# Rows sent to their experts place by place: POOL's later sends held until PE has turned the rows of an earlier expert

## The reference, cut to what matters

```python
x = x + L0_xattn(layernorm(x), ...)          # int8-like quantised expert linear
x = x + L0_ffn(layernorm(x), ...)            # weights looked up in a table of 16
x = x + L1_xattn(ctx, layernorm(x), ...)     # a state-space scan
x = x + L1_ffn(layernorm(x), ...)            # mixture of experts, below

probs = softmax(x @ gate_w)                  # 32 experts; 2048 rows
w, sel = top_k(probs, 8);  w = w / sum(w)
# every row goes to its 8 experts; an expert takes its rows in order, up to its capacity
y = (silu(xg @ w_gate[e]) * (xg @ w_up[e])) @ w_down[e]
out[row] += w * y
```

## Time and profile before

| | us |
|---|---|
| timed runs, median of 3 | 2109.94 |
| timed runs, lowest and highest | 2106.46, 2112.08 |
| the profiled execution, its own time | 2116.83 |
| the profiled execution, its span | 2115.0 |
| routing, sends and experts (last block) | 1225 to 2115 |
| POOL's 128 sends, first and last start | 1258.5, 1431.6 |
| PE busy, DVE busy, ACT busy, POOL busy | 1535.6, 1441.8, 903.5, 679.5 |

### The profile page before, as it was taken

One profiled execution on the slowest core, in us unless ns is written; L12 is line 12 of the kernel. 1 busy time (PEld: TensorE's weight loads), 2 busy tenths in 40 slices (PEclk: granted clock), 3 DMA queues, 4 the chain that ended last, 5 costly groups with the idle time before them and its releaser, 6 DMA issues. The chain is left out here.

```text
span 2115.0 us, 26326 instructions
## 1 busy us (share of the span) xinstructions
PE 1535.6 (73%) x9312; PEld 1305.2 (62%) x9312; DVE 1441.8 (68%) x2096; ACT 903.5 (43%) x1579; POOL 679.5 (32%) x450
## 2 busy tenths in 40 slices
PE   5767787774599699699689352106999999998930
PEld 3444454443589589589689341105888899997820
DVE  6676786864898998998999362003666655558854
ACT  3535555453444544544544140003655566665510
POOL 1010100101544644654554136770000000008876
PEclk9879788976699799799799775557999999999965
DMA  7888798744637338437435045654668666669877
GB/s 226 290 284 299 243 360 306 270 145 146 249 130 292 150 125 295 162 117 277 167 131 179 20 166 203 248 209 134 199 200 287 209 210 210 210 209 329 271 220 232
DMA packets 167496, 455.04 MB, mean 215 GB/s; under 512 B 17328, under 2 KB 19376, under 8 KB 157632
## 3 DMA queue, kind: packets, MB, share of 16 engines
q1 hardware_dynamic: 90880, 280.11, 39.7%
q10 hardware_dynamic: 56000, 106.06, 13.6%
q0 software_dynamic: 20480, 67.13, 9.3%
HBM read 271.83 MB, written 181.40 MB: 214 GB/s over the span
## 5 line engine op out<-in xcount | busy, mean ns | idle before, releaser
L1116 POOL TENSOR_TENSOR mix_st<-mix_Bb,mix_du 128x2048 f32<-128x2048 f32 x64 | 293.2, 4582 | 272.0 <-DVE mix_st L1399 260.2
L1391 DVE TENSOR_TENSOR_SCAN mix_st<-mix_dA,mix_st 128x512 f32<-128x512 f32 x256 | 311.9, 1218 | 42.8 <-POOL mix_st L1116 22.2
L1800 POOL DMA_INDIRECT moe_gat<-x_by_expert,moe_where x128 | 160.8, 1256 | 509.9 <-DMA x_by_expert<-moe_ys 471.5
L1264 ACT ACTIVATE mix_dA<-mix_dt,mix_A 128x512 f32<-128x512 f32 x256 | 177.0, 692 | 263.6 <-DVE mix_st L1391 259.8
L1187 PE MATMUL mix_G<-mix_xThi,mix_wup 128*128 128x256 f32 x1408 | 266.0, 287 | 15.6 <-issue 14.7
L1924 PE MATMUL moe_G<-moe_xhi,moe_whi 128*128 128x288 f32 x768 | 234.9, 306 | 11.0 <-issue 11.0
L1187 PEld LDWEIGHTS mix_G<-mix_xThi,mix_wup 128*128 128x128 f32 x1408 | 226.6, 196 | 18.5 <-issue 17.1
L1924 PE MATMUL moe_G<-moe_xhi,moe_wlo 128*128 128x288 f32 x768 | 229.1, 298 | 9.6 <-issue 9.6
L1924 PE MATMUL moe_G<-moe_xlo,moe_whi 128*128 128x288 f32 x768 | 229.4, 299 | 9.0 <-issue 8.9
L427 PE MATMUL front_L<-front_oh,front_pick 128*128 128x512 f32 x528 | 176.1, 470 | 45.4 <-ACT front_wst L574 28.9
L1213 PE MATMUL mix_Y<-mix_ident,mix_st 128*128 128x128 f32 x1024 | 145.9, 298 | 86.4 <-DVE mix_st L1399 86.3
(11 more groups left out here) (235 smaller groups left out, 3238.6 us busy)
## 6 DMA issues: line engine op xcount, KB each, us to landing
x_by_expert<-front_zeros ACTq DMA_DIRECT2D x16, 4096.0 KB, 20.4
mix_wup<-w_halves SPq DMA_DIRECT2D x44, 1024.0 KB, 5.6
moe_raw<-in_ew SPq DMA_DIRECT2D x32, 1280.0 KB
moe_xt<-x_by_expert SPq DMA_DIRECT2D x128, 256.0 KB
x_by_expert<-moe_ys ACTq DMA_DIRECT2D x128, 256.0 KB
mix_wdn<-w_halves SPq DMA_DIRECT2D x44, 512.0 KB, 6.5
front_idx<-in_idx SPq DMA_DIRECT2D x44, 384.0 KB, 8.6
w_halves<-front_wst SPq DMA_DIRECT2D x44, 384.0 KB, 7.5
```

Of the source, the lines that this page charges most:

```text
L1116: nc.gpsimd.tensor_tensor(st[:, g % STBUF, :, :], Bb[:, q, :, :], du[:, k % 2, :].unsqueeze(1).to_broadcast([P, NG, S]), ALU.mult).then_in ...
L1264: nc.scalar.activation(dA[:, :], dt[:, k % 2, :], ACT.Exp, scale=A[:, c, m:m + 1]).then_inc(da_ready, 1)
L1391: nc.vector.tensor_tensor_scan(r, dA[:, :], r, 0.0, ALU.mult, ALU.add).then_inc(scanned, 1)
L1800: pool.indirect_dma_start(out=gat[:, q, :], out_offset=None, in_=s["XG"], in_offset=bass.IndirectOffsetOnAxis(ap=where[:, i, k:k + 1], axi ...
```

## The change

Ahead of the 16 sends of each place k from 2 to 7, POOL now waits for `xT_ready` to reach NT * (k - 1), which is when PE has transposed all five tiles of expert k-2: 5 for place 2, 10 for place 3, up to 30 for place 7. Nothing else is changed: the sends, their order, the loads and PE's stream are the same.

```diff
--- before.py
+++ after.py
@@ -1784,6 +1784,7 @@
                     for i in range(b * TT, (b + 1) * TT):
                         send(i, k)
             for k in range(2, TOP):
+                pool.wait_ge(xT_ready, NT * (k - 1))
                 for i in range(TILES):
                     send(i, k)
```

## The result

The changed kernel took 2055.6 us (median of 4, 2052.18 to 2062.63) beside 2111.01 us for the kernel before on the same chip: ratio 0.9734, 95% interval 0.9712 to 0.9755, some 55 us less. Forecast were 2081 us and 29 us less, so the gain is nearly twice the forecast one. Two later batches gave the same: 2061.97 beside 2116.06 (0.9733, 0.9710 to 0.9756) and 2063.12 beside 2114.9 (0.9761, 0.9717 to 0.9805).

What follows compares the result with a forecast made beforehand. PE's results, known only one in 2.8 us while POOL sends without a break, bound the kernel. M5 = 1341 + 35.6 + 4 x 33.6 = 1511, 29 us earlier; 2109.94 - 29 = 2081 us, own range 2050 to 2107, over the cases 2015 to 2116.

Steps and rivals of the forecast that it cites:

- M5: Middle of period 5, PE's 64-row transposes: forecast 1511 against 1539.9 before, 29 us earlier; nothing different after it.
- The first rival: POOL's sends: each has its price wherever it stands; M5 = 1543, +3 us, time 2113; no change had 0.14.
- The tail after every burst: Between a place's last send and PE's release stand 12 us, five times: +21 us, 2131; chance 0.14.
- Hardly touched PE: Short bursts at the gathers' price, 22 us a period: M5 = 1451, 89 us earlier, 2021; chance 0.17.
- M0: Middle of period 0, PE's 64-row transposes after place 2's sends: forecast 1341, 107 us before the old one.
- The five periods: PE's work from M0 to M5, places 3 to 7 sent one each: first 35.6 us, then four of 33.6.
- 6 us of full pace: Grace after each start of a place's sends: PE does 40 instructions before its results come late.
- the long train: POOL's unbroken sends in the kernel before, 147 us: PE's results become known one in 2.8 us.
- catching up, tail and dependency: After a place's burst: 8.6 us for PE's remaining work, 2 us tail, 1 us for a dependency not ready.
- The clock: PE after each stop runs at the low clock: 24 matmuls in 5.00 us at 0.56.
- The Trainium skill's rule: DMAs from all engines share 16 DMA engines; held sends cost the same at another time, nothing won.
- a cost of recording the execution: If the hold were only this, the timed kernel would be some 100 us shorter than the profiled; no chance given.

Runs made afterwards that it cites:

- the floor: Kernel before without the 96 sends of places 2 to 7 and the loads' waits for them: 1982.67 us beside 2111.0.
- the pairs: Changed kernel with the holds of places 3, 5 and 7 taken out, so three groups of 32 sends: 2086.71 us beside 2111.0 (0.9880).
- the breaks: Kernel before, no holds, twenty small POOL clears ahead of each place from 2 to 7: 2058.97 us beside 2114.9; in another batch 2026.27 beside 2001.54.
- the plain DMAs: Kernel before with the 96 sends of places 2 to 7 as plain POOL DMAs of one block each, no holds: 2003.07 us beside 2111.0.
- in order: Kernel before, indirect sends of places 2 to 7 with row numbers in order to scratch: 2001.09 us beside 2001.54; later 2117.93 beside 2116.06.

## Why the prediction was right, and where it was not

**The mechanism.** PE's results become known late while POOL sends its indirect DMAs without a break, and a break ends that: shown, by the floor (128 us come back without the sends), by the pairs and by the breaks. The rest of the kernel follows M5 with nothing added: shown by equal PE work behind it.

**The first rival, a fixed price for each send,** is out: 82 and 11 instructions in the two halves of one group, and 2087 with three holds against 2056 with six.

**The tail after every burst** didn't come. After place 5's last send 3 to 4 us went by, the 2 us that I took with the send's own landing. **Hardly touched PE** is out too; a period is 29.3 us on the mean, not 22.

**What was mis-sized.** M0 was forecast for 1341 and came at 1331.9, of which 2.6 us are the earlier start. The five periods were forecast at 35.6 and 33.6 us, 170 together, and took 30.8, 26.3, 33.8, 26.7 and 29.0, 146.7 together. That is 9 + 23 of the 32 us by which M5 came earlier than 1511. The term that was mis-sized is the rate inside a group: I took 6 us of full pace and then one result in 2.8 us, the value of the long train. In place 5's group it was 0.4 and then 0.8 us a result up to the end; 2.8 is what a train reaches when it runs on. PE started 90 instructions in a group on the mean of five, where I had 76 all told, the 30 issued ahead included. So less was left behind each group. I had 11.6 us from the 22.0 us of a burst to the middle, catching up, tail and dependency together; it was 3.2, 3.5, 11.0, 3.9 and 6.2. How much of that is the pace and how much the other terms was not separated. At M0 it was the same term: I had PE's results flow again 22.0 us after the first send and 3.5 us more to the middle, and the middle came 17.8 us after it. Three groups of matmuls and four of the five tiles had started by 1323.4; only the fifth tile was late, behind 7.20 us of idle time.

The clock was sized about right. Behind each stop PE restarts at the lower level, as forecast:

```profile
1410.00:1416.00 6.00, 3.95 (x16) 3.62 (x16) 3.65 (x6) 3.03 (x7) 0.00 (x0) 0.50 0.60 191
1416.00:1422.90 6.90, 5.42 (x32) 4.39 (x31) 6.18 (x10) 3.24 (x7) 0.00 (x0) 0.93 0.91 316
```

The granted clock is 0.50 behind place 5's group and 0.93 after it; from 1412.67 on 21 instructions start within 4.7 us, near the 24 in 5.0 us that I charged.

**The Trainium skill's rule.** The Trainium skill, page "DMA: Bandwidth & Descriptors", section "Issuing engines are not separate DMA queues", would, as the prediction read it, have the held sends win nothing, as the same transfers at another time. The transfers are the same here too, and 55 us were won; by the plain DMAs, which filled the DMA engines and held nobody, the loss isn't one of their bandwidth.

**The gain by number:** 61.3 us at M5, 2.6 of them from before the change, and 3.3 more by the end of the span, of which I have no cause. The time of 2055.6 lies in the range and in the forecast's own range of 2050 to 2107, near its lower end.

**What stays open.** It is open what it is in POOL's indirect DMAs that delays the counts of PE. It isn't bytes or DMA load (plain writes), nor scattered rows (in order). It depends on the pace (1.93 us is harmless) and on how long the train runs. Whether indirect reads do it was tried only where nothing was late. And I don't know why one batch had none of it. The difference shows already in the first burst, whose sends are the same in every run: there ACT's copy came 16.3 to 22.9 us after the first send in every traced run of the four batches, and 12.8 to 13.4 us in the fifth.

One rival was put aside too early: that the delay is a cost of recording the execution. The prediction set the profiled execution, 2116.83 us, beside the timed ones, 2109.94. But the record gives a span and a granted clock for each timed execution of the experiments, and the profiled one is counted among them; so none of these times is known to be free of recording, and their agreement speaks neither way. The steps in the trace would fit such a cost. In the second half of the group of places 4 and 5 (fewer holds) PE's matmuls start at

```profile
1403.43 0.40 PE L1926 MATMUL moe_G<-moe_xhi,moe_wlo 128*128 128x288 f32 x1 [1.52 <-issue]
1405.54 0.40 PE L1926 MATMUL moe_G<-moe_xhi,moe_whi 128*128 128x288 f32 x1 [1.71 <-issue]
1406.23 0.60 PE L1926 MATMUL moe_G<-moe_xlo,moe_whi 128*128 128x288 f32 x1 [0.29 <-issue]
1407.62 0.40 PE L1926 MATMUL moe_G<-moe_xhi,moe_wlo 128*128 128x288 f32 x1 [0.79 <-issue]
1408.32 0.40 PE L1926 MATMUL moe_G<-moe_xhi,moe_whi 128*128 128x288 f32 x1 [0.30 <-issue]
```

that is 2.11, 0.69, 1.39 and 0.70 us apart, each close to a multiple of 0.70 (two starts shortly before are 0.39 and 0.34 apart); and the 2.80 us of the long train are four such steps for one weight load and one matmul, as if the start and the end of each had its price. That is argued from the steps alone. No run shows it, and if it is so, the 55 us would be won only where an execution is recorded.

## What to carry to other kernels

When an engine issues a long train of indirect DMAs, look in the trace at how late the other engines' results become known, not at the DMA engines' share; if the delay grows along the train, breaks of a few microseconds can pay: here six of about 5 us won 56 us. Measure the floor first by leaving the train out: it says what there is to win, here 128 us, of which the holds took 55. Ask also whether the delay is there in an execution that nothing records, which was not settled here. And run a version like this in several batches, since the stall that it avoids was absent in one of five, and there breaks of the same length cost 25 us.

## What the runs showed of the hardware that was not expected

- PE's results became known one in 2.80 us, whatever the size of the matmul, beside unbroken indirect DMAs at 1.28 us each; in a group of 16 between breaks it was 0.4 to 0.8 us. In the unbroken train the weight loads and matmuls of PE start 1.40 us apart, and in a train of 32 many of their steps are close to 0.70 us or a multiple of it.
- Plain DMAs from the same queue moved 401 GB/s beside a PE that was busy 55.36 of 60 us.
- The same kernel on the same chip number took 2001.09 and 2117.93 us in two batches; within a batch the kernel before never strayed by more than 0.5%.
